# Self-attention scores of a decoder in float32r, as value and rest, with the keys made one batch ahead

## The reference

```
q, k, v = x @ Wq.T + bq, x @ Wk.T + bk, x @ Wv.T + bv            # (8, 256, 16 heads, 16)
s[b,h,i,j] = (q[b,h,i] . k[b,h,j] + q[b,h,i] . rel_k[clip(j-i)]) / 4
p = softmax(s, axis=j)
o[b,h,i] = sum_j p[b,h,i,j] * (v[b,h,j] + rel_v[clip(j-i)])
x = layernorm(x + o @ Wo.T + bo)
```

## Time and profile before

| | us |
|---|---|
| median of 3 runs | 854.18 |
| lowest, highest | 852.06, 854.31 |
| the profiled execution, its own time | 854.72 |
| its span, first to last instruction | 852.9 |
| TensorE, VectorE, ScalarE, GpSimd busy in it | 805.5, 654.1, 609.7, 427.7 |

### The profile page before, as it was taken

The page is one execution under the profiler, slowest core; times in us unless marked ns, Lnnn a source line. Parts: engine busy times, 40 slices in busy tenths (PEclk is TensorE's granted clock), DMA queues, the critical chain, the costliest instruction groups (busy, mean ns, idle before and its releaser), DMA issues.

```text
span 852.9 us, 20803 instructions
## 1 busy us (share of the span) xinstructions
PE 805.5 (94%) x6837; PEld 605.5 (71%) x6837; DVE 654.1 (77%) x2466; ACT 609.7 (71%) x1595; POOL 427.7 (50%) x459
## 2 busy tenths in 40 slices
PE   9998999999999988999999999999999999999996
PEld 8876776766667766677777767667766777677785
DVE  4987778888998766777777667673888888985667
ACT  4547887888784367877877777774899999985341
POOL 2255667666644155254552534224665666425763
PEclk9999999999999999999999999999999999999999
DMA  9401761112103368977868688756122211100001
GB/s 321 157 25 45 224 194 51 55 60 81 70 15 124 124 216 269 295 218 242 277 205 268 215 247 255 239 177 212 42 66 67 66 66 66 64 2 1 26 25 50
DMA packets 105392, 115.64 MB, mean 136 GB/s; under 512 B 28589, under 2 KB 93869, under 8 KB 105030
## 3 DMA queue, kind: packets, MB, share of 16 engines
q1 hardware_dynamic: 104724, 113.97, 41.8%
q10 hardware_dynamic: 562, 0.35, 0.1%
HBM read 48.70 MB, written 51.82 MB: 118 GB/s over the span
## 4 chain that ended last, share of the span: by engine, by line
PE 46%; ACT 9%; DVE 5%; issue 3%; DMA 2%; POOL 1%; SPq 0%; DVEq 0%; ACTq 0%; POOLq 0%
PE bank L1544 7%; PE bank L242 6%; PE bank L250 4%; PE bank L2259 4%; PE bank L1559 3%; PE bank L2245 3%; ACT bias_area L2597 2%; PE bank L2276 2%; PE bank L1528 2%; PE bank L1585 2%; PE bank L1595 2%; PE bank L2309 2%; PE bank L2353 2%; PE bank L2347 2%; ACT Sx L1750 2%
## 5 line engine op out<-in xcount | busy, mean ns | idle before, releaser
L242 PE MATMUL bank<-x_feat,w_all_mats 128*128 128x256 f32 x384 | 92.7, 386 | 1.8 <-ACT q_full L358 0.6
L2994 POOL TENSOR_TENSOR bnd<-bnd,consts 128x60 f32<-128x60 f32 x64 | 18.1, 305 | 142.0 <-DMA bnd<-band_scratch 142.0
L242 PEld LDWEIGHTS bank<-x_feat,w_all_mats 128*128 128x128 f32 x384 | 70.5, 191 | 14.3 <-ACT rw L2639 3.8
L2597 ACT ACTIVATE bias_area<-bias_area,mq_two 128x256 f32<-128x256 f32 x128 | 66.2, 529 | 0.0
L1003 DVE COPY q_heads<-bank 128x512 f32<-128x512 f32 x64 | 42.0, 684 | 24.4 <-PE bank L717 24.4
L2773 DVE COPY q_heads<-bank 128x512 f32<-128x512 f32 x64 | 41.2, 683 | 23.2 <-PE bank L2259 23.2
L896 ACT ACTIVATE Sx<-Sx,mq 128x256 f32<-128x256 f32 x128 | 54.4, 498 | 5.4 <-DVE mq L995 5.4
L1750 ACT ACTIVATE Sx<-Sx,mq 128x256 f32<-128x256 f32 x128 | 54.3, 500 | 3.4 <-DVE mq L1848 3.4
L904 ACT ACTIVATE q_heads<-bank 128x512 f32<-128x512 f32 x64 | 37.8, 590 | 26.3 <-PE bank L717 26.3
L1856 DVE COPY q_heads<-bank 128x512 f32<-128x512 f32 x64 | 42.0, 684 | 17.0 <-PE bank L1544 17.0
L896 ACT ACTIVATE Pr<-Pr,mq 128x256 f32<-128x256 f32 x128 | 54.4, 502 | 0.9 <-DVE mq L995 0.9
(11 more groups left out here) (309 smaller groups left out, 2384.8 us busy)
## 6 DMA issues: line engine op xcount, KB each, us to landing
dist<-skew_scratch SPq DMA_DIRECT2D x64, 296.0 KB, 4.1
skew_scratch<-rw SPq DMA_DIRECT2D x30, 588.0 KB, 4.5
bnd<-band_scratch SPq DMA_DIRECT2D x64, 108.0 KB, 2.6
band_scratch<-bias_area SPq DMA_DIRECT2D x32, 162.0 KB, 2.5
band_scratch<-bias_area SPq DMA_DIRECT2D x32, 148.0 KB, 2.1
skew_scratch<-dist SPq DMA_DIRECT2D x4, 1024.0 KB, 7.1
context_values<-dist SPq DMA_DIRECT2D x8, 512.0 KB, 2.6
v_two<-context_values SPq DMA_DIRECT2D x8, 512.0 KB, 4.3
```

The source lines that it names most:

```text
L242: last = pe.matmul(dst[:, m * S:(m + 1) * S], w[:, k, m * P:(m + 1) * P], rhs[:, k, :], start=(k == 0), stop=(k == FT - 1))
L2597: last = act.activation(rows_of(n, g)[:, t, :], rows_of(n, g)[:, t, :], ACT.Exp, bias=mq_two[:, n % 2, g, t:t + 1], scale=-1.0, accum_out= ...
```

## The change

The scores of batches 1 to 7 of the self-attention take the form of the first cross-attention. Batch 0 keeps float32, with k in the new tile `spare`.

- Within each row group of 32 partitions, the features of two heads now alternate (weights, biases, `rel_k` and the 0/1 columns are laid out so beforehand). Even partitions belong to one head, odd ones to the other. `q_cells` holds q for the two heads, `k_cells` two tiles each for them. The partitions of a head hold the value part; those of the neighbour are filled with the rest part of the same head by SyncE (`turn_q`: two transfers, `turn_k`: four, 128 KB each). The two products of a group, with `k_value` and `k_rest`, are summed in the bank: 16 float32r products in the place of eight float32 ones.
- `split_q` on GpSimd writes the rounded value twice in one cast and then the rest `q_low`.
- `copy_k` on VectorE writes, from the projection's bank, both copies of the value (two instructions) and, after a wait for them, both copies of the rest (two more). Only then is `m_bank` free.
- In round 2 of TensorE the ternary product moves behind turns 0 and 1. In batch 0, `project_k(1)` moves ahead of `turn(0, 2)` and `project_v(0)`, with a wait for `copy_k(1)` ahead of `project_v(0)`; on VectorE `copy_k(1)` moves from iteration j = 1 to the end of j = 0.
- The tile `spare` takes 14 KB of each partition of SBUF; the program reserves 1,024 bytes in each for descriptors instead of the default.

```diff
@@ scores @@
-                        if j == 0:
-                            pe.wait_ge(k_sb, b + 1)
-                        pe.wait_ge(q_split, FT * b + j % 2 + 1)
+                        if n == 0:
+                            pe.wait_ge(k_sb, 1)
                         ge(pe, s_max, TT * 4 * n)
+                        if b == 0:
+                            pe.wait_ge(q_split, j % 2 + 1)
+                        elif j == 0:
+                            pe.wait_ge(q_turned, 16 * 2 * b)
+                            pe.wait_ge(k_turned, 16 * 4 * b)
                         for t in range(TT):
-                            for g in range(4):
-                                r = slice(32 * g, 32 * (g + 1))
-                                last = pe.matmul(s_bank[g][:, t * S:(t + 1) * S],
-                                                 q_par[r, b % 2, j % 2, j // 2, t * P:(t + 1) * P],
-                                                 k_two[r, b % 2, j // 2, :], start=True, stop=True)
+                            for i in range(2 if b else 1):
+                                for g in range(4):
...
+                                        last = pe.matmul(s_bank[g][:, t * S:(t + 1) * S],
+                                                         q_cells[b % 2][r, j % 2, j // 2, q],
+                                                         k_cells[b % 2][i][r, j % 2, j // 2, :],
+                                                         start=(i == 0), stop=(i == 1))
@@ first_round @@
                             if b == 0:
                                 pe.wait_ge(r_sb, 4 + 1)
+                                project_k(1)
+                                turn(n, 2)
+                                pe.wait_ge(k_sb, 2)
...
                         if b == 0:
-                            pe.wait_ge(k_sb, 2)
+                            pe.wait_ge(r_sb, 4 + 2)
                             turn_normed(2)
@@ second_round @@
                         if b < B:
                             scores(n + 1)
+                        if b < B:
+                            turn(n, 0)
+                            turn(n, 1)
                         if b + FF_EARLY < B:
...
                             ternary_product(b + FF_EARLY)
-                        if b < B:
-                            turn(n, 0)
-                            turn(n, 1)
@@ copy_k @@
+                        value, rest = k_cells[b % 2]
                         ge(dve, s_mm, NQ * (b - 1))
+                        both = lambda m: m_bank[:, m * S:(m + 1) * S].unsqueeze(1).broadcast_to([P, 2, S])
                         for m in range(FT):
-                            last = dve.tensor_scalar(k_two[:, b % 2, m, :], m_bank[:, m * S:(m + 1) * S],
-                                                     kb[:, m:m + 1], None, ALU.add)
+                            last = dve.tensor_scalar(value[:, :, m, :], both(m), kb[:, m:m + 1], None, ALU.add)
+                        last.then_inc(k_high_made, 1)
+                        dve.wait_ge(k_high_made, b)
+                        for m in range(FT):
+                            last = dve.scalar_tensor_tensor(out=rest[:, :, m, :], in0=both(m), scalar=kb[:, m:m + 1],
+                                                            in1=value[:, :, m, :], op0=ALU.add, op1=ALU.subtract)
                         last.then_inc(k_sb, 1)
@@ VectorE's loop @@
+                            if j == 0 and b == 0:
+                                copy_k(1)
                             if j == 0 and 1 <= b < B - 1:
                                 invert(b - 1)
...
-                            if j == 1 and b < B - 1:
+                            if j == 1 and 1 <= b < B - 1:
                                 copy_k(b + 1)
@@ SyncE @@
+                    def turn_k(b):
+
+                        sp.wait_ge(k_sb, b + 1)
+                        value, rest = (c[:, :, :, :].bitcast(F32) for c in k_cells[b % 2])
+                        sp.dma_start(value[1:P:2, 0, :, :], rest[0:P:2, 0, :, :]).then_inc(k_turned, 16)
+                        sp.dma_start(rest[1:P:2, 0, :, :], value[0:P:2, 0, :, :]).then_inc(k_turned, 16)
+                        sp.dma_start(value[0:P:2, 1, :, :], rest[1:P:2, 1, :, :]).then_inc(k_turned, 16)
+                        sp.dma_start(rest[0:P:2, 1, :, :], value[1:P:2, 1, :, :]).then_inc(k_turned, 16)
...
                             if n >= 2 and n + 2 < NQ * B:
                                 load_dist(n + 2)
+                            if j == 0 and b < B - 1:
+                                turn_q(b + 1)
+                            if j == 1 and b < B - 1:
+                                turn_k(b + 1)
```

More of the change, by code:

```diff
@@ L54 @@
         "rel_v_last",
-        "x0_bv0", "x0_bv1", "sa_bv0", "sa_bv1", "x1_bv0", "x1_bv1"] + [f"head{i}" for i in range(8)] + ["half0", "half1"] + ["pair0", "pair1"]
+        "x0_bv0", "x0_bv1", "sa_bv0", "sa_bv1", "x1_bv0", "x1_bv1"] + [f"head{i}" for i in range(8)] + ["pair0", "pair1"]
 ROWS = ["x0_bo", "sa_bo", "x1_bo"]
@@ L3234, in lay_out @@
     for c in "qk":
-        for short, long in (("x0", "L0_xattn"), ("x1", "L1_xattn")):
+        for short, long in (("x0", "L0_xattn"), ("sa", "L1_attn"), ("x1", "L1_xattn")):
             mats[f"{short}_W{c}"] = mats[f"{short}_W{c}"][:, paired]
@@ L3241, in lay_out @@
     for i in range(8):
-        col[f"head{i}"] = (np.arange(P) // DH == i).astype(np.float32)
+        col[f"head{i}"] = (np.arange(P) // 32 * 2 + np.arange(P) % 2 == i).astype(np.float32)
     for i in range(2):
-        col[f"half{i}"] = (np.arange(P) // DH % 2 == i).astype(np.float32)
         col[f"pair{i}"] = (np.arange(P) % 2 == i).astype(np.float32)
@@ L3279, in lay_out @@
         "gate_up": np.stack([w["L1_ffn_w_gate"].T, w["L1_ffn_w_up"].T]), "down": mat(w["L1_ffn_w_down"]),
[L3280 removed]
+        "ident": np.eye(P, dtype=np.float32), "rel_k": rel_k.T[np.arange(P) % 32 // 2],
         "rel_v": rel_parts, "mix": mix, "consts": consts,
```

48 lines of the change are left out of this document (41 added, 7 removed).

## The result

| | median, us | runs |
|---|---|---|
| before | 854.24 | 852.06 to 854.35, 4 runs |
| after | 866.31 | 864.48 to 866.79, 4 runs |

The ratio is 1.0142, 95% interval 1.0126 to 1.0159: the change costs 12 us. The profiled execution of the changed kernel took 866.79 (span 865.0), against 854.72 (span 852.9) before. VectorE is busy 669.5 us instead of 654.1, TensorE 805.0 instead of 805.5.

A forecast was written before the change was run, and what follows sets the result against it. TensorE bounds steady batches, except where VectorE or ScalarE sets the pace. Steady batches 0.0, first batch +5.9 and clock +1.7 make +7.6: 862.3 us profiled, 861.8 median; range 856.5 to 868, 8 in 10.

The forecast's parts named there:

- The scores: Score groups of batches 1 to 7: 0.40 us less each, at most 11.2 us over 28 groups.
- First batch and clock: Batch 0: the new order lengthens one chain by 5.9 us, and a clock fall behind TensorE's wait adds 1.7.
- the clock's term: Behind TensorE's gap in batch 0: 3.4 us of work at half speed, +1.7 us, from a possible 0 to 3.4.
- The 3.5 us wait: Sign in the profile after: TensorE waits about 3.5 us near 317 for VectorE's q_heads copy.
- scores(3) at 336 to 338: Sign in the profile after: this score group starts at 336 to 338 instead of 330.01; before 333 refutes the forecast.
- copy_k in round 2: VectorE's key copy takes 2.8 us, 1.9 more; mix_heads is 0.6 late in batches 1 to 4, 0.2 in 5 and 6.
- What is hidden: GpSimd's split_q was counted at nothing, its reader coming a whole batch later; SyncE's added transfers were expected in time.
- Round 1: Steady batches: the shorter score group gains nothing, because VectorE sets the gates behind it.
- The crowded queue: Rival: added transfers delay later dist loads, one us per batch, 7 us more than forecast, 869; chance 0.12.

The follow-up runs named there:

- e3: Changed kernel with scores of batches 1 to 7 as 8 float32 products on the value cells, the neighbour's rests left out: 869.13 us, ratio 1.0170.
- e10: Changed kernel with GpSimd's two query instructions held until VectorE's three quantiser instructions are done, same place in GpSimd's order: 865.76 us, ratio 1.0144.
- e5: Changed kernel with VectorE's two key rest instructions left out from the keys of batch 3 on, so old rests are used: 865.45 us, ratio 1.0130.
- e9: Changed kernel with the ternary product ahead of the two turns in round 2 again: 866.20 us, ratio 1.0149.
- e1: Changed kernel with batch 0 in its old order (key projection, third turn and key copy of batch 1 back in place): 861.94 us, ratio 1.0082.
- e4: Changed kernel without the six transfers per batch between neighbouring partitions: 865.17 us, ratio 1.0123.
- e7: Changed kernel with batch 0 and ternary product in old order, one plain key copy by VectorE, value and rests by GpSimd: 855.60 us, ratio 1.0021.
- e2: Changed kernel with 17 idle products on TensorE in the 3.6 us gap of batch 0: 865.01 us, ratio 1.0122.

## Why the prediction was right, and where it was off

The direction and the time were right within 4.5 us; the sum was 862.3 of one execution, which took 866.79. In the traces the 4.5 us between them are 2.3 ahead of the self-attention and 3.6 more in rounds 2 and 4 than forecast, less 1.1 that rounds 1 gave and 0.3 behind group 31. By its own steps:

- **The scores** fell by 0.40 us per group, as the row of the first attention said; by the rule of 4 passes ("FP8 and Floating Point Precision", section "TensorE Precision Notes" in the Trainium skill) the prediction's estimate was 0.58 us for the rows of a group, and the trace doesn't agree (they span 0.75, from 435.69 to 436.44, and the next row starts after 0.68, as in the earlier trace rows). Only round 3 keeps it: shown by e3.
- **First batch and clock**: forecast 5.9 + 1.7 = 7.6, measured 7.6, on the chain 5.8 + 1.7. The 5.9 is shown, as e10's chain gives 5.8 too. That the clock's term fits to a tenth is luck: it was a choice between 0 and 3.4, and in five other traces of the same instructions the stretch grew by 8.7, with 2.9 for the clock in e10. The prediction's reading that the clock fell once in the trace of before is not quite right either: it is at 0.50 again at 850 to 852, where TensorE does nothing any more; the sum doesn't hang on it. The 3.5 us wait and scores(3) at 336 to 338 (339.93, or 337.6 less the 2.3 of ahead) were as said.
- **copy_k in round 2**: 2.86 us (2.8 forecast), ready 1.97 us after the group (1.94 forecast). The term that was mis-sized is what follows: mix_heads 0.95 late instead of 0.6, because `add_ff` starts 2.67 us after the group and not 2.44, and mix_heads 0.70 behind the end of the last q_heads copy and not 0.5; 0.35 more in each of four batches, 0.1 in batches 5 and 6 and in batch 7. e5 and e9 showed that I had also read the place too simply: the key copy and the moved ternary product each are enough to lose the round.
- **"What is hidden"** failed: I counted GpSimd's `split_q` at nothing, since its reader comes a batch later. Its cost is not to its reader but to its neighbour. Rounds 4 of batches 1 to 3 cost 1.8 us over before, and with the two instructions held (e10) nothing of it is left; this is shown by traces, not by the time of e10. The size varies: in e1 to e5 and e9, with the same instructions there, it is 0.7 to 2.7 us. The step counted who waits for the result and not who runs beside it.
- **Round 1** was forecast at nothing and gave 1.1 us, in batches 1, 5 and 7; I have no experiment on why.
- **Ahead of the self-attention** 2.3 us were lost where no instruction changed. In 12 further traces group 0 starts at 306.7 to 308.9 (before 308.07, after 310.41), so this is the one execution, not the change.
- **The crowded queue** is excluded by e4 at its price of 7 us, though the key transfers landed after 3.3 us and more and not 2.1.
- **In sum**, what the traces give for an execution like the five (8.7 for the first batch, 2.9 for the steady ones, -0.7 behind group 31, most of which is the last round 3 and which is otherwise not explained) is 10.9 of the 12.1 us by the medians.

## What to carry to other kernels

Ask of a moved operation not only who waits for its result but what runs beside it and what is queued behind it, on SyncE's queue too. A faster product is worth only the rounds in which TensorE sets the pace: 7 of 28 here. Undoing one of two parallel causes can show nothing; undo both before either is cleared.

## What the runs showed of the hardware

- **VectorE beside GpSimd.** The same instruction on 128x512 took 0.43 us with GpSimd held (e10) and 1.38 beside its subtraction. In the rows of round 4 above each slow instruction ends 0.28 us behind GpSimd's: 384.03 against 383.75, 385.45 against 385.17. This fits the Trainium skill, "SBUF — State Buffer", section "Who interferes with whom": between GpSimd and an instruction of VectorE in a 2-port mode, which `tensor_scalar` can enter, whoever issues first has the shared port pair for the whole instruction, and the other waits. (No trace shows the mode.) But in the kernel before the rule doesn't fit: GpSimd's two multiplications stood in the same place, from 371.51 to 374.78 in batch 1, and VectorE's three, from 371.94 on, took 0.53, 0.86 and 0.79 us. So not every instruction of GpSimd blocks as long; which do wasn't measured alone.
- **The clock falls in some executions and not in others where nothing differs.** Ten microseconds ahead of anything that the change touches, busy time by stretch, kernel before:

```profile
285.00:295.00 10.00, 9.89 (x53) 7.92 (x54) 6.57 (x19) 4.26 (x9) 0.85 (x2) 0.83 0.11 29
```

After:

```profile
285.00:295.00 10.00, 9.11 (x39) 6.65 (x40) 5.40 (x18) 2.31 (x4) 0.84 (x2) 0.66 0.11 42
```

e4:

```profile
285.00:295.00 10.00, 9.54 (x58) 7.42 (x59) 7.88 (x21) 5.07 (x10) 0.85 (x2) 1.00 0.10 29
```

Mean clocks of 0.83, 0.66 and 1.00 are 3.4, 6.8 and 0 us at 1.2 GHz. Nor is the length of a wait a safe sign: in e7 the clock fell behind 1.12 us of it at 375.95 and stayed at 1.00 behind 1.36 us at 341.30, and in e2 it fell although the 3.6 us gap was filled with products.
